# A segment sum over 400,000 edges: eight chunks moved from gathering to counting, and one operation for three weight parts

## Chip, cores and metric

One core of a Trainium2 chip runs the whole kernel. The metric is device time in microseconds (us). Of the kernel before, three timed runs gave 4982.99, 4986.41 and 4995.05; the median is 4986.41.

## What is computed

A graph has 12,500 nodes with 64 features and 400,000 edges, sorted by their target `dst`. Every edge brings a message to its target: the source node's features times `node_w`, plus the edge's own 64 attributes times `review_w`, both times the edge's weight. The messages are summed by target, added to the node, and the result is normalised over its 64 features.

```python
h = feat_src @ node_w.T
rf = review_feat @ review_w.T
m = (h[src_idx] + rf) * edge_w
out = segment_sum(m, dst_idx, num_segments=N_DST)
x = layernorm(x + out, axis=-1)
```

The two matrix products are linear, so the kernel sums the weighted raw features by target first and multiplies the 12,500 sums by the weights at the end.

## The kernel before

The edges are cut at `COUNTED_FROM`. Those ahead of it are *gathered*, those behind it are *counted*; the two ways run interleaved on the same engines.

**Gathered: 88 chunks of 3200 edges** (25 tiles of 128). For a chunk SyncE (SP) loads `src`, `dst`, the weights and the edge attributes, and GpSimd (POOL) issues 25 indirect DMAs (`gather_chunk`, L366), each of which fetches the 256-byte rows of x for 128 edges into `rows`. Four slots of `rows` are in use, so the gather of chunk c + 4 starts when VectorE has freed the slot of chunk c. VectorE makes for each of the 25 tiles a weighted one-hot over 128 targets (`scatter`, L441), and TensorE multiplies `rows` by it, 25 fp32 products into one *window* of PSUM (`window_ps`, L839; each has two passes in the trace, so 50 matmuls). VectorE adds the window to `sums` (L453).

**Counted: 925 tiles of 128 edges in 52 groups** of 18 tiles (7 in group 0). No row of x is fetched. For each tile VectorE makes two one-hots: `hot_key` (L495, 128 x 686), which says which block of 128 nodes the source lies in and which of seven target slots the edge goes to, and `hot_lo` (L497), the source's place within its block, times the edge's weight. The weight is cut in three bf16 parts W0, W1 and W2, so `hot_lo` has three planes of 128 x 128. TensorE multiplies them: six bf16 matmuls of 343 columns for a tile (L881), which leaves in `count_ps` how much of every node each target slot gets. There are two such PSUM buffers and three buffers for the one-hots. ScalarE copies `count_ps` to `counts` (L744). At the group's end TensorE multiplies `counts` by the table of x held in SBUF (`sum_x`, L896, 98 products or 196 matmuls), ScalarE reads the result (`x_sums`, L759, once in a group), and two small products and an addition (L904, L905, L911, L531) bring the group's 126 slots into `sums`.

**Preparing a group.** `prepare` packs key, low part and weight parts of 18 tiles in rows of `packed`; TensorE turns them into columns in the middle of the sum over x of the group before (`turn_cols`, L855 to L859); ScalarE copies them to `cols` (L728); then VectorE's `begin_hot` makes `hot_rel` (L510, L514) and the first three hot tiles of the next group. W0 comes from `g_w` and stands last in `cols`.

**Order.** Each engine's program is written out by hand in steps, and a hardware loop runs over rounds of them. One step has one group and one or two chunks. TensorE's order in a step is: window of the first chunk, `turn_slots`, the 18 counting tiles, window of the second chunk if there is one, `multiply_slots`, sum over x. `STEPS = (2, 1, 2, 1, 2)` gives the chunks of a round's five steps; nine rounds are run, then six steps with two chunks (`LAST_STEPS`), two more chunks, and the last two (`LATE_CHUNKS`). On VectorE the hot tiles of the next group's start stand ahead of the scatter of the next step's first chunk. The last stage multiplies `sums` by the weights in 15 blocks of up to eight rows of 128 nodes, adds x, normalises and stores; the blocks that the last two chunks can reach come late.

Of the kernel before, what the change touches and what calls it, by code (L numbers as in the profile page):

```python
# [25 lines left out]
ALU = mybir.AluOpType  # L26
# [8 lines left out]
P = 128  # L35
# [7 lines left out]
GT = 18  # L43
HOT_BUFS = 3
SPAN = 7
CHUNKS = 88
STEPS = (2, 1, 2, 1, 2)
LAST_STEPS = (2, 2, 2, 2, 2, 2)
LATE_CHUNKS = 2
LN_EPS = 1e-5  # L50

# [1 line left out]
def build(nc, x, src, dst, attr, weight, node_w, review_w, out):  # L53
# [4 lines left out]
    GROUP = GT * P  # L58
    COUNTED_FROM = CHUNKS * CHUNK
    COUNTED = (EDGES - COUNTED_FROM) // P  # L60
# [4 lines left out]
    HI = (NODES - 1) // P + 1  # L65
# [23 lines left out]
    blocks = [(h, until - h) for h, until in zip(edges, edges[1:])]  # L89
    BLOCKS = len(blocks)  # L90
# [4 lines left out]
    BY_P = NODES // P  # L95
    G_DST_DMAS = 1 + (GT - 1) // GT0 + 1

    with ExitStack() as ctx:
# [20 lines left out]
        x_tab = sb("x_tab", [P, HI, F])  # L119
# [4 lines left out]
        hi_lo = sb("hi_lo", [GT, 2, P], I32)  # L124
        tile_first = sb("tile_first", [GT, 1])
        w_cut = sb("w_cut", [GT, 2, P], BF16)
        KEY, LO, W1, W2, REL, W0 = range(6)
        packed = sb("packed", [GT, W0, P])
        cols = sb("cols", [P, W0 + 1, GT])
        slot_rel = sb("slot_rel", [NS, 1])  # L130
# [3 lines left out]
        hot_lo = [sb(f"hot_lo{b}", [P, 3, P], BF16) for b in range(HOT_BUFS)]  # L134
# [8 lines left out]
        count16 = sb("count16", [P, HI * SPAN], F16)  # L143
# [109 lines left out]
        stored = sem("stored")  # L253
# [53 lines left out]
        @block.sync  # L307
        def _(sp):
            def load_src(c, s):
                sp.dma_start(src_sb[s][:, :], by_partition(src, c)).then_inc(src_landed[s], 16)  # L310

            def load_rest(c, s):
                sp.dma_start(dst_sb[s][:, :], by_partition(dst, c)).then_inc(edge_landed[s], 16)
                sp.dma_start(w_sb[s][:, :], by_partition(weights, c)).then_inc(edge_landed[s], 16)
                sp.dma_start(rows[:, s, :, F:2 * F],
                             attr[bass.ds(c * CHUNK, CHUNK), :].rearrange("(p k) f -> p k f", k=TILES)
                             ).then_inc(edge_landed[s], 16)

            def load_chunk(c, s, r):

                sp.wait_ge(slot_free[s], r + 1)
                load_src(c, s)
                load_rest(c, s)

            for s in range(SLOTS):
                load_src(s, s)
            sp.dma_start(dst_i[:, 0, :], dst.rearrange("(c e) -> c e", e=CHUNK)).then_inc(dst_loaded, 16)

            sp.dma_start(g_dst[1:GROUPS, :, :], dst[COUNTED_FROM + GT0 * P:EDGES].rearrange(
                "(g t e) -> g t e", t=GT, e=P)).then_inc(g_dst_loaded, 16)  # L330
            for t0 in range(0, GT, GT0):
                n = min(GT0, GT - t0)
                sp.dma_start(g_dst[0:1, t0:t0 + n, :], dst[COUNTED_FROM:COUNTED_FROM + n * P].rearrange(
                    "(a t e) -> a t e", a=1, e=P)).then_inc(g_dst_loaded, 16)
            sp.dma_start(w_both[:, 0:F], node_w).then_inc(w_loaded, 16)
            sp.dma_start(w_both[:, F:2 * F], review_w).then_inc(w_loaded, 16)
            for s in range(SLOTS):
                load_rest(s, s)
            each_chunk(sp, SLOTS, CHUNKS, load_chunk)

            sp.wait_ge(tables_ready, 1)
            with sp.If(is_narrow(sp) == 0):
                each_chunk(sp, CHUNKS, ALL_CHUNKS, load_chunk)
            for n, b in enumerate(early + late):
                h0, j = blocks[b]
                if n < ACT_BLOCKS:
                    sp.wait_ge(act_scaled, n + 1)
                else:
                    sp.wait_ge(pool_scaled, n - ACT_BLOCKS + 1)
                whole = min(j, BY_P - h0)  # L350
                sp.dma_start(out[h0 * P:(h0 + whole) * P, :].rearrange("(h l) f -> l h f", l=P),
                             x_tab[:, h0:h0 + whole, :]).then_inc(stored, 16)
                if whole < j:
                    sp.dma_start(out[BY_P * P:NODES, :], x_tab[0:NODES - BY_P * P, BY_P, :]).then_inc(stored, 16)
            sp.wait_ge(stored, 16 * (BLOCKS + (BY_P < HI)))

        @block.gpsimd
        def _(pool):
# [50 lines left out]
        def _(dve):  # L409
# [77 lines left out]
            def make_hot(g, tiles):  # L487

                n0 = tiles_before(g)
                for t in tiles:  # L490
                    h = t % HOT_BUFS

                    if t >= HOT_BUFS:
                        dve.wait_ge(counted, n0 + t - HOT_BUFS + 1)
                    dve.tensor_scalar(hot_key[h][:, :], count16[:, :], cols[:, KEY, t:t + 1], None, ALU.is_equal)  # L495
                    for i, part in enumerate((W0, W1, W2)):
                        made = dve.tensor_scalar(hot_lo[h][:, i, :], count16[:, 0:P], cols[:, LO, t:t + 1],  # L497
                                                 cols[:, part, t:t + 1], ALU.is_equal, ALU.mult)
                    made.then_inc(hot_ready, 1)

            def begin_hot(g):
# [146 lines left out]
            for a in range(2):  # L648
                made = dve.tensor_scalar(w_t[:, a * F:(a + 1) * F], w_t_ps[:, 0:F], w_mean[:, 0:1], None, ALU.subtract)
# [352 lines left out]
```

## Time and profile before

| | us |
|---|---|
| median of three timed runs | 4986.41 |
| profiled execution, span of the core | 4978.1 |
| TensorE matmuls busy | 2706.6 (54%) |
| TensorE weight loads busy | 2036.4 (41%) |
| VectorE busy | 1848.4 (37%) |
| ScalarE busy | 832.4 (17%) |
| GpSimd busy | 2097.5 (42%) |
| mean granted clock of TensorE | 0.722 of full speed |

The timed median lies 8.3 us above the span. In the rows, an instruction or a group of merged ones stands with its start, its length, and in brackets the idle time of its engine ahead of it with what ended that. A matmul's end is modelled, its start is recorded. "issue" means that the profile shows nothing for which the engine waited, "remote" that the releasing instruction isn't among the records.

### The profile page before, as it was taken

To read this page: it belongs to the slowest core of one execution; us is meant where nothing else is said; L and a number is where in the kernel's file an instruction comes from. 1 tells how busy PE (TensorE), PEld (TensorE's weight loads), DVE (VectorE), ACT (ScalarE), POOL (GpSimd) and SP (SyncE) were. 2 spreads that over 40 slices of the span, in tenths; PEclk is the share of its full clock that TensorE was granted. 3 is DMA by queue.
4 is the path that set the end of the run, shared out by engine and by line. 5 is a ranking of instruction groups with operands and counts; after the bars stand their busy time and mean duration, and the time that the engine had idled before them with its cause. 6 is when DMAs were issued, how large, how long until landed. Compare 5 with 4: busy or idle time off the path is not lost.

```text
span 4978.1 us, 63532 instructions
## 1 busy us (share of the span) xinstructions
PE 2706.6 (54%) x22003; PEld 2036.4 (41%) x22004; DVE 1848.4 (37%) x7016; ACT 832.4 (17%) x1327; POOL 2097.5 (42%) x2223
## 2 busy tenths in 40 slices
PE   0555555545655545555456555555554556455465
PEld 0343444434443434444344434344443444344345
DVE  3333333423442333333334424333333344333344
ACT  0111111111121111121111211111111112111112
POOL 7343343443334443444433344434444333544432
PEclk9776777767776767777667767677776777667677
DMA  4111121111111111211111211112111112112111
GB/s 98 37 34 37 34 42 38 34 36 38 37 38 38 34 35 38 41 38 34 35 38 35 42 37 35 34 38 42 38 34 35 37 36 42 37 34 43 36 35 38
DMA packets 531458, 192.11 MB, mean 39 GB/s; under 512 B 489893, under 2 KB 495772, under 8 KB 530975
## 3 DMA queue, kind: packets, MB, share of 16 engines
q1 hardware_dynamic: 334128, 80.80, 8.6%
q0 software_dynamic: 70400, 72.23, 6.6%
q10 hardware_dynamic: 126623, 34.94, 3.2%
q8 instruction: 198, 3.24, 0.3%
q14 instruction: 109, 0.89, 0.1%
HBM read 184.60 MB, written 3.20 MB: 38 GB/s over the span
## 4 chain that ended last, share of the span: by engine, by line
PE 43%; another core or an unknown queue 28%; issue 21%; DVE 4%; ACT 2%; DVEq 1%; ACTq 1%; POOLq 0%; POOL 0%
PE x_sums_ps L896 15%; PE count_ps L881 15%; PE window_ps L839 11%; ACT counts L744 2%; DVE scatter L441 1%; DVE hot_lo L497 1%; PE attr_ps L873 1%; ACTq L771 0%; PE turn_ps L858 0%; PE turn_ps L855 0%; DVEq L422 0%; DVEq L425 0%; DVE hot_key L495 0%; PE count_ps L924 0%
## 5 line engine op out<-in xcount | busy, mean ns | idle before, releaser
L366 POOL DMA_INDIRECT rows<-x,src x2200 | 2088.8, 949 | 2791.5 <-DMA src<-src 2146.3
L881 PE MATMUL count_ps<-hot_key,hot_lo 128*128 128x343 bf16 x5550 | 1157.4, 361 | 1294.2 <-ACT counts L744 839.0
L896 PE MATMUL x_sums_ps<-counts,x_tab 128*64 128x126 f32 (+1 forms) x10192 | 865.5, 302 | 790.2 <-issue 775.0
L881 PEld LDWEIGHTS count_ps<-hot_key,hot_lo 128*128 128x128 bf16 x5550 | 570.1, 113 | 1726.5 <-issue 1092.5
L896 PEld LDWEIGHTS x_sums_ps<-counts,x_tab 128*64 128x64 f32 x10192 | 692.5, 154 | 948.4 <-issue 927.3
L744 ACT ACTIVATE counts<-count_ps 128x686 f32<-128x686 f32 x925 | 737.3, 802 | 1784.9 <-remote 1335.6
L495 DVE TENSOR_SCALAR hot_key<-count,cols 128x686 bf16<-128x686 f16 x925 | 377.8, 408 | 1550.8 <-remote 1272.3
L441 DVE TENSOR_SCALAR scatter<-column,dst_left,w 128x128 f32<-128x128 f32 x2200 | 588.3, 347 | 576.2 <-PE window_ps L839 503.0
L497 DVE TENSOR_SCALAR hot_lo<-count,cols 128x128 bf16<-128x128 f16 x2775 | 721.7, 323 | 4.9 <-issue 4.9
L839 PE MATMUL window_ps<-scatter,rows 128*128 128x128 f32 x4400 | 563.1, 289 | 85.2 <-issue 55.4
L839 PEld LDWEIGHTS window_ps<-scatter,rows 128*128 128x128 f32 x4400 | 535.0, 200 | 120.9 <-issue 108.8
L510 DVE TENSOR_TENSOR hot_rel<-column,cols 128x126 f32<-128x126 f32 (+1 forms) x52 | 15.2, 292 | 645.1 <-issue 441.8
L873 PEld LDWEIGHTS attr_ps<-hot_rel,g_attr 128*128 128x128 f32 x926 | 189.0, 228 | 45.1 <-issue 9.5
L726 ACT ACTIVATE slot_rel<-turn_ps,slot_no 126x1 f32<-126x1 f32 (+1 forms) x52 | 13.6, 262 | 979.2 <-remote 625.3
L873 PE MATMUL attr_ps<-hot_rel,g_attr 128*128 128x14 f32 x926 | 155.2, 243 | 12.6 <-remote 12.6
L759 ACT ACTIVATE x_sums<-x_sums_ps 128x126 f32<-128x126 f32 (+1 forms) x52 | 14.3, 276 | 881.9 <-PE x_sums_ps L896 881.9
L734 ACT ACTIVATE slot_rows<-x_sums_ps 126x128 f32<-126x128 f32 x52 | 14.4, 278 | 400.8 <-PE x_sums_ps L905 400.8
L448 DVE TENSOR_SCALAR dst_left<-dst_left 128x25 f32<-128x25 f32 x88 | 15.8, 180 | 146.8 <-PE window_ps L839 146.8
L531 DVE TENSOR_TENSOR sums<-sums,turn_ps 128x128 f32 x52 | 15.0, 289 | 76.2 <-PE turn_ps L911 43.0
L430 DVE TENSOR_SCALAR dst_left<-dst,lo_all 128x25 f32<-128x25 int32 x88 | 22.3, 254 | 50.2 <-issue 50.2
L405 POOL TENSOR_TENSOR x_tab<-x_tab,counts 128x512 f32<-128x512 f32 (+2 forms) x8 | 5.9, 748 | 79.7 <-DVE counts L573 79.6
L855 PE MATMUL turn_ps<-tile_first,spread 18*126 18x1 f32 (+1 forms) x104 | 19.4, 253 | 33.7 <-DVE packed L484 33.7
(112 smaller groups left out, 557.5 us busy)
## 6 DMA issues: line engine op xcount, KB each, us to landing
rows<-edge_attr SPq DMA_DIRECT2D x88, 800.0 KB
rows<-x,src POOLq DMA_INDIRECT x2200
g_attr<-edge_attr ACTq DMA_DIRECT2D x51, 576.0 KB
out<-x_tab SPq DMA_DIRECT2D x11, 256.0 KB
counts<-dst SPq DMA_DIRECT2D x1, 1562.5 KB
src<-src SPq DMA_DIRECT2D x88, 12.5 KB, 1.7
dst<-dst SPq DMA_DIRECT2D x88, 12.5 KB
w<-edge_weight SPq DMA_DIRECT2D x88, 12.5 KB
```

Source lines behind the costliest of these rows:

```text
L366: pool.indirect_dma_start(out=rows[:, s, k, 0:F], out_offset=None, in_=x, in_offset=bass.IndirectOffsetOnAxis(ap=src_sb[s][:, k:k + 1].bit ...
L430: dve.tensor_scalar(dst_left[:, :], dst_sb[s][:, :], lo_all[:, bass.ds(c, 1)], None, ALU.subtract).then_inc(left_ready, 1)
L441: made = dve.tensor_scalar(scatter[:, q % PART_BUFS, i, :], column[:, :], dst_left[:, k:k + 1], w_sb[s][:, k:k + 1], ALU.is_equal, ALU.mult)
L448: dve.tensor_scalar(dst_left[:, :], dst_left[:, :], float(WIN), None, ALU.subtract).then_inc(left_ready, 1)
L495: dve.tensor_scalar(hot_key[h][:, :], count16[:, :], cols[:, KEY, t:t + 1], None, ALU.is_equal)
L497: made = dve.tensor_scalar(hot_lo[h][:, i, :], count16[:, 0:P], cols[:, LO, t:t + 1], cols[:, part, t:t + 1], ALU.is_equal, ALU.mult)
L744: act.activation(counts[:, :, t * SPAN:(t + 1) * SPAN].rearrange("p (a h) d -> p a h d", a=2), count_ps[t % 2][:, :, 0:HALF].rearrange("p ...
L839: done = pe.matmul(window_ps[:, 0:WIN], rows[:, s, k, :], scatter[:, q % PART_BUFS, i, :], start=(k == 0), stop=(k == TILES - 1))
L855: pe.matmul(turn_ps[0:nt * SPAN, REL_COL:REL_COL + 1], spread[0:nt, 0:nt * SPAN], tile_first[0:nt, 0:1], start=True, stop=True)
L873: pe.matmul(attr_ps[0:(until - t) * F, t * SPAN:until * SPAN], g_attr[:, t:until, :].rearrange("p t f -> p (t f)"), hot_rel[:, t:until, :] ...
L881: last = pe.matmul(count_ps[b][:, a, 0:HALF], hot_lo[h][:, i, :], hot_key[h][:, a * HALF:(a + 1) * HALF], start=(i == 0), stop=(i == 2))
L896: done = pe.matmul(x_sums_ps[half * F:(half + 1) * F, 0:ns], x_tab[:, hi, :], counts[:, hi, 0:ns], start=(hi < 2), stop=(hi >= HI - 2))
```

## The change

`CHUNKS` goes from 88 to 80: 200 of the 2200 gather instructions go, and 1125 tiles are counted in 63 groups (9 tiles in group 0) where 925 were in 52. The steps of a round become ten with 12 chunks, eight of them with one chunk; with 63 groups the loop runs six rounds, and two steps of two chunks follow. The columns are reordered so that W1, W2 and W0 lie side by side, and the three `tensor_scalar` that made the planes of `hot_lo` become one `scalar_tensor_tensor` over 3 x 128 elements: the counter spread over the planes is compared with the low part and multiplied by the weight part of the plane, spread over 128 elements. The late blocks become rows 59 to 64, the last block is row 97 alone, and the store skips an empty range.

```diff
-CHUNKS = 88
-STEPS = (2, 1, 2, 1, 2)
-LAST_STEPS = (2, 2, 2, 2, 2, 2)
+CHUNKS = 80
+STEPS = (1, 1, 1, 1, 2, 1, 1, 1, 1, 2)
+LAST_STEPS = (2, 2)
...
-        KEY, LO, W1, W2, REL, W0 = range(6)
+        KEY, LO, REL, W1, W2, W0 = range(6)
...
                 whole = min(j, BY_P - h0)
-                sp.dma_start(out[h0 * P:(h0 + whole) * P, :].rearrange("(h l) f -> l h f", l=P),
-                             x_tab[:, h0:h0 + whole, :]).then_inc(stored, 16)
+                if whole:
+                    sp.dma_start(out[h0 * P:(h0 + whole) * P, :].rearrange("(h l) f -> l h f", l=P),
+                                 x_tab[:, h0:h0 + whole, :]).then_inc(stored, 16)
...
                     dve.tensor_scalar(hot_key[h][:, :], count16[:, :], cols[:, KEY, t:t + 1], None, ALU.is_equal)
-                    for i, part in enumerate((W0, W1, W2)):
-                        made = dve.tensor_scalar(hot_lo[h][:, i, :], count16[:, 0:P], cols[:, LO, t:t + 1],
-                                                 cols[:, part, t:t + 1], ALU.is_equal, ALU.mult)
+                    made = dve.scalar_tensor_tensor(
+                        hot_lo[h][:, :, :], count16[:, 0:P].unsqueeze(1).to_broadcast([P, 3, P]), cols[:, LO, t:t + 1],
+                        cols[:, W1:W0 + 1, t].unsqueeze(2).to_broadcast([P, 3, P]), ALU.is_equal, ALU.mult)
                     made.then_inc(hot_ready, 1)
```

## Rows read from the trace of the kernel before

**Rows 1.** The page, costliest groups: busy us, mean ns of one, idle before.

```profile
L366 POOL DMA_INDIRECT rows<-x,src x2200 | 2088.8, 949 | 2791.5 <-DMA src<-src 2146.3
L881 PE MATMUL count_ps<-hot_key,hot_lo 128*128 128x343 bf16 x5550 | 1157.4, 361 | 1294.2 <-ACT counts L744 839.0
L495 DVE TENSOR_SCALAR hot_key<-count,cols 128x686 bf16<-128x686 f16 x925 | 377.8, 408 | 1550.8 <-remote 1272.3
L497 DVE TENSOR_SCALAR hot_lo<-count,cols 128x128 bf16<-128x128 f16 x2775 | 721.7, 323 | 4.9 <-issue 4.9
```

**Rows 2.** Stretches of one step: length, PE, PEld, DVE, ACT, POOL busy (count), clock, DMA.

```profile
2108.40:2139.60 31.20, 10.45 (x58) 6.03 (x56) 7.98 (x30) 5.62 (x7) 23.69 (x25) 0.65 0.26 52
2139.60:2152.80 13.20, 10.10 (x50) 6.36 (x50) 6.33 (x24) 6.54 (x9) 0.00 (x0) 0.65 0.01 3
2152.80:2165.50 12.70, 11.80 (x204) 11.37 (x204) 7.62 (x33) 1.54 (x6) 0.00 (x0) 1.00 0.24 51
```

**Rows 3.** The same view, a gather over the sum over x.

```profile
2058.00:2091.00 33.00, 10.77 (x92) 6.51 (x89) 9.19 (x36) 0.41 (x2) 23.97 (x25) 0.63 0.24 51
```

**Rows 4.** ScalarE's reads of x_sums: timeline of one round, then all, then the last.

```profile
1989.11 0.28 ACT L759 ACTIVATE x_sums<-x_sums_ps 128x126 f32<-128x126 f32 x1 [21.80 <-PE x_sums_ps L896]
...
2098.92 0.28 ACT L759 ACTIVATE x_sums<-x_sums_ps 128x126 f32<-128x126 f32 x1 [27.51 <-PE x_sums_ps L896]
...
2165.26 0.28 ACT L759 ACTIVATE x_sums<-x_sums_ps 128x126 f32<-128x126 f32 x1 [5.11 <-PE x_sums_ps L896]
...
2269.75 0.28 ACT L759 ACTIVATE x_sums<-x_sums_ps 128x126 f32<-128x126 f32 x1 [23.14 <-PE x_sums_ps L896]
...
2337.19 0.28 ACT L759 ACTIVATE x_sums<-x_sums_ps 128x126 f32<-128x126 f32 x1 [5.11 <-PE x_sums_ps L896]
...
2443.57 0.28 ACT L759 ACTIVATE x_sums<-x_sums_ps 128x126 f32<-128x126 f32 x1 [21.34 <-PE x_sums_ps L896]
...
L759 ACT ACTIVATE x_sums<-x_sums_ps x52: 213/277/278, 156.3 to 4891.9; 128x126 f32<-128x126 f32 x51, 128x49 f32<-128x49 f32 x1
...
L759 ACT ACTIVATE x_sums<-x_sums_ps x7: 277/277/278, 4267.0 to 4891.9; 128x126 f32<-128x126 f32 x7
```

**Rows 5.** Timeline of TensorE, first window of a round.

```profile
2447.85 8.05 PE L839 MATMUL window_ps<-scatter,rows 128*128 128x128 f32 x50 [4.32 <-issue]
```

**Rows 6.** Timeline: window behind a two-chunk step; then hot tiles, scatter, window behind one-chunk.

```profile
2099.33 5.84 PE L839 MATMUL window_ps<-scatter,rows 128*128 128x128 f32 x50 [0.45 <-issue]
...
2160.82 0.40 DVE L495 TENSOR_SCALAR hot_key<-count,cols 128x686 bf16<-128x686 f16 x1
...
2161.79 0.40 DVE L495 TENSOR_SCALAR hot_key<-count,cols 128x686 bf16<-128x686 f16 x1
...
2164.02 6.50 DVE L441 TENSOR_SCALAR scatter<-column,dst_left,w 128x128 f32<-128x128 f32 x25
...
2165.78 6.17 PE L839 MATMUL window_ps<-scatter,rows 128*128 128x128 f32 x50 [0.56 <-DVE scatter L441]
```

**Rows 7.** Groups by shape: scalar_tensor_tensor of the last stage, and an operand spread by zero steps.

```profile
L514 DVE TENSOR_TENSOR hot_rel<-hot_rel,cols 128x126 f32<-128x126 f32 x51 | 15.0, 293 | 1.7
...
L549 DVE SCALAR_TENSOR_TENSOR x_tab<-x_total,x_tab 128x512 f32<-128x512 f32 x11 | 8.0, 726 | 0.9 <-DVE sums L531 0.9
...
L549 DVE SCALAR_TENSOR_TENSOR x_tab<-x_total,x_tab 128x192 f32<-128x192 f32 x2 | 0.7, 349 | 0.0
```

**Rows 8.** Timeline of clear counting: ScalarE's reads and VectorE's hot_key.

```profile
2044.93 0.80 ACT L744 ACTIVATE counts<-count_ps 128x686 f32<-128x686 f32 x1 [0.22 <-PE count_ps L881]
2044.93 0.40 DVE L495 TENSOR_SCALAR hot_key<-count,cols 128x686 bf16<-128x686 f16 x1
...
2045.94 0.80 ACT L744 ACTIVATE counts<-count_ps 128x686 f32<-128x686 f32 x1 [0.21 <-PE count_ps L881]
```

**Rows 9.** Timeline of the head: VectorE under the first gathers, a tile's count behind them.

```profile
81.63 0.31 DVE L497 TENSOR_SCALAR hot_lo<-count,cols 128x128 bf16<-128x128 f16 x1 [1.11 <-issue]
...
146.35 1.90 PE L881 MATMUL count_ps<-hot_key,hot_lo 128*128 128x343 bf16 x6
```

More of the change, by code:

```diff
@@ L350, in _ @@
                 whole = min(j, BY_P - h0)
-                sp.dma_start(out[h0 * P:(h0 + whole) * P, :].rearrange("(h l) f -> l h f", l=P),
-                             x_tab[:, h0:h0 + whole, :]).then_inc(stored, 16)
+                if whole:
+                    sp.dma_start(out[h0 * P:(h0 + whole) * P, :].rearrange("(h l) f -> l h f", l=P),
+                                 x_tab[:, h0:h0 + whole, :]).then_inc(stored, 16)
                 if whole < j:
                     sp.dma_start(out[BY_P * P:NODES, :], x_tab[0:NODES - BY_P * P, BY_P, :]).then_inc(stored, 16)
-            sp.wait_ge(stored, 16 * (BLOCKS + (BY_P < HI)))
+            sp.wait_ge(stored, 16 * (sum(h0 < BY_P for h0, _ in blocks) + (BY_P < HI)))
         @block.gpsimd
```

## Prediction, made before the changed kernel was run

> **What bounds the kernel now.** I began with the page's parts 1 and 5. No engine is near full: the gathers of GpSimd (POOL) are 2200 instructions, 25 for a chunk, each 0.95 us, and TensorE's counting matmuls, the next line, are busy for 1157 us [rows 1]. A mean over the run hides the point, so the second view is the table of stretches through one step. Under a chunk's gather (31.2 us) TensorE starts 58 matmuls; in the 13.2 us behind it 50; in the 12.7 us of the sum over x 204 [rows 2]. A gather that falls on the sum over x does the same: 92 matmuls in 33 us [rows 3]. So the time is made of two kinds of stretch: clear ones, and those under a gather, in which TensorE almost stands still whatever its work is. Why it stands the trace doesn't say; that it does is enough for the sum.
>
> The third view gives the price list. ScalarE reads x_sums once in a group, so the distance between two such reads is one step [rows 4]. The round shown goes two, one, two, one, two chunks: 109.8, 66.3, 104.5, 67.4 and 106.4 us. I take 67.0 for a one-chunk step. The first step of a round holds the loop's branch: TensorE is idle for 4.32 us there and the window takes 8.05 us [rows 5], against 5.84 us, 0.41 us behind the x_sums read, in an ordinary step [rows 6]; that is 5.9 us a round. Nine rounds last from 156.3 to 4267.0, 456.7 each, which leaves (456.7 - 134.0 - 5.9) / 3 = 105.6 for a two-chunk step; the six two-chunk steps behind the loop take 104.15 each [rows 4]. A chunk's marginal price is therefore 38.6 us (about 6 of window and 32 of standstill), a group's 28.4.
>
> **The mix of steps.** The changed kernel has 6 rounds of eight one-chunk and two two-chunk steps, then two two-chunk steps. At the prices above a round is 8 x 67.0 + 2 x 105.6 + 5.9 = 753.1, the whole 4518.6 + 208.3 = 4726.9. Before, the same stretch is 4735.6 (156.3 to 4891.9) [rows 4]. So the exchange alone is worth -8.7: eight chunks and three loop passes out (-309 and -18), eleven groups in (+313), and four of the cheaper steps behind the loop become steps of a round (+6). 200 gather instructions go, and so do eight chunks' loads on SP's queue; ScalarE's queue gets the loads of eleven more groups. Both queues issue beside TensorE's work, in steps of unchanged length, so I cost them at nothing; were one of them late, the stretch behind it would grow, and I have no sign of that in a one-chunk step.
>
> **A price that the list hides.** Every one-chunk step of before follows a two-chunk step, whose long sum over x gives VectorE time to make the hot tiles and the scatter ahead. Of the new kernel's 48 one-chunk steps 36 follow a one-chunk step. There VectorE is late: it gets the columns in the middle of the sum over x, makes three hot tiles at 0.97 each, and starts the scatter at 2164.02; TensorE's window ends 6.69 us after the x_sums read (start at 2165.78, 6.17 long). Behind a two-chunk step it is 0.41 + 5.84 = 6.25 [rows 6]. That is +0.44 for 36 steps: +15.8.
>
> **The one operation.** For each tile three tensor_scalar become one scalar_tensor_tensor over 384 elements. The four operations of a tile take 0.97 us start to start, though their durations add up to 1.38 (0.41 and three of 0.32): each overlaps the next by 0.10 [rows 1, 6]. So the three cost 0.67. The nearest rows of the new operation have 192 elements (0.349 us) and 512 (0.726) [rows 7]; on a line between them 384 take 0.575, less 0.10 of overlap 0.47. The bounds are the two rows, 0.25 and 0.63. The operand spread by a step of zero costs nothing that shows: hot_rel's two such operations take 0.29 us [rows 7]. I take 0.47, a saving of 0.20 a tile.
>
> What is it worth? Not VectorE's 0.20 x 1125 us. In a clear counting stretch ScalarE's reads follow each other at 1.01 us, each 0.80 long, and VectorE's hot_key starts at the same instant as the read: it too waited for TensorE's `counted` [rows 8]. The pace is TensorE's tile, then ScalarE's read, with two PSUM buffers; VectorE, at 0.97, has just enough time. A faster VectorE changes nothing there, nor under a gather, where TensorE is the late one. The saving counts only where VectorE's queue runs into the scatter. Before a window that follows a one-chunk step it brings the scatter forward by 3 x 0.20 = 0.6, of which TensorE can use what its own pace leaves, 6.17 - 5.84, and hardly more: 0.35. That is 48 steps (36 and the 12 two-chunk ones behind a one-chunk step): -16.8. Before the second window of a two-chunk step only one tile's saving counts, 14 x 0.2 = -3. With the upper bound, 0.63, the windows would gain 0.12 each, -6 in all. With the lower they gain no more than with 0.47.
>
> VectorE: DVE Perf Modes of the Trainium skill (The perf-mode tier table, and the errata table above it) speaks against this edit: a one-source bf16 operation may run four results a cycle, a two-source one at most two and in fp32 one, and its formula gives 0.28 us for the three operations and 0.46 for the new one. By it VectorE would lose 0.18 a tile, and the windows 48 x 0.54 = 26 us where I have a gain of 17. The measured 0.67 for the three contradicts the first figure; no row here shows the new form.
>
> **Head and tail.** Group 0 has 9 tiles for 7. It ends behind the first four gathers, when a tile costs TensorE 1.9 us [rows 9]: +4. The order of columns (REL ahead of W1) moves nothing. The blocks of the last stage stay 15, two of them late with six rows for five; at most 2 us, taken as 0. The store of an empty block is skipped.
>
> **Sum.** -8.7 + 15.8 - 19.8 + 4 = -8.7. The profiled execution (4978.1) becomes 4969.4. The median of the timed runs lies 8.3 above the span, which I keep: 4978.
>
> **Rivals.**
> 1. *VectorE is part of the standstill* (faster). At the head, under the first gathers, a hot_lo starts after 1.11 us of idle that nothing in the profile explains [rows 9]. If that happens in the steps too, two instructions fewer a tile shorten each standstill: 1 us for 62 groups, 4916. Against it: in the steps VectorE starts each time with the release by TensorE.
> 2. *The one operation is slower than the three* (slower). It decides from 0.70 us: then VectorE needs more than the 1.01 of a tile. At twice the slope of the rows, 384 x 2 x 1.18 ns is 0.9, less overlap 0.8: nine clear tiles of 62 groups pay 0.10 each, 56, the windows 48 x 0.4 = 19, and the gain of 20 is gone: 5073. The page named above would put the slowing at the windows alone, 5024. For it: bf16 and fp16 operands, which no scalar_tensor_tensor row has. Against: 0.726 for 512 elements.
> 3. *A chain of one-chunk steps is dearer than its pieces*, as the loads of a group then come every 67 us without a pause. From +0.5 us for each of 48 steps the kernel is slower by 0.3%; at +0.8, 5016.
> 4. *The one operation does not save anything*: +20 on the sum, 4998, still within 0.3%.
>
> **How the numbers follow.** About 0.3% (15 us) is what a measurement of this kernel can tell from no change. My sum: 0.57, between 4960 and 4994, of which 0.18 below 4971. Rival 1: 0.19, 4895 to 4960. Rival 2: 0.08. Rival 3: 0.10, of which 0.08 beyond 0.3%. Rival 4: 0.06. So faster 0.37, same 0.47, slower 0.16. The likeliest case's own range is 4960 to 4994; for 8 in 10 it has to reach into rivals 1 and 3: 4935 to 5008.
>
> **What would show it.** One-chunk steps of 67.0 to 67.4 between x_sums reads, two-chunk ones of 105; six idle stretches of about 4 us instead of nine; the new operation at 0.55 to 0.6 us long and the period of hot_key ahead of a window at 0.77; the window behind a one-chunk step at 5.9 instead of 6.17; the reads in clear counting still at 1.01. The prediction is wrong if that last pace moves, if a chunk's standstill is not 29 to 32 us any more, or if the one-chunk step leaves 66.5 to 67.8: 0.3 us there is 14 us in all.

## The result, and the profile after

The changed kernel takes 4740.57 us (median, 4733.61 to 4764.11), the kernel before 4989.44 beside it: a ratio of 0.951 (0.949 to 0.954). The forecast was 4978, with 4935 as its lower end. The change is faster by 249 us where I had summed up 9.

In later runs the kernel before took 4924 to 4993 us on three chips of this kind and 2814 to 2819 us on three others, so each run below is read against the kernel before on its own chip, and "with the standstill" or "without it" says which kind of chip it was.

The page of the changed kernel, two of its costliest groups (busy us, mean ns of one, idle before) and its chain; the first two answer to [rows 1]:

```profile
L367 POOL DMA_INDIRECT rows<-x,src x2000 | 1988.2, 994 | 2673.1 <-DMA src<-src 2086.4 <-issue 586.7
...
L497 DVE SCALAR_TENSOR_TENSOR hot_lo<-count,cols 128x384 bf16<-128x384 f16 x1125 | 686.4, 610 | 0.0
...
PE 56%; another core or an unknown queue 22%; issue 16%; ACT 4%; DVE 2%; DVEq 0%; POOL 0%; ACTq 0%; POOLq 0%
```

The new operation lasts 0.61 us. The line to look at is the first: the same gather instruction, with the same work, now lasts 994 ns where it lasted 949. Nobody had touched it.

One step of the changed kernel (one chunk behind one chunk), under its gather, behind it, and in the sum over x; columns as in [rows 2]:

```profile
core 0: us, PE busy (x) PEld busy (x) DVE busy (x) ACT busy (x) POOL busy (x), PEclk, DMA share, GB/s
2158.63:2191.22 32.59, 16.83 (x89) 9.70 (x89) 11.31 (x24) 9.63 (x12) 25.27 (x25) 0.68 0.25 49
2191.22:2200.37 9.15, 5.94 (x26) 3.73 (x26) 1.76 (x7) 3.40 (x6) 0.00 (x0) 0.50 0.04 10
2200.37:2211.84 11.47, 11.47 (x202) 11.27 (x198) 6.23 (x24) 0.41 (x2) 0.00 (x0) 0.98 0.24 54
```

The gather is 1.4 us longer than in [rows 2], and TensorE starts 89 matmuls under it where it started 58. What is left for the stretch behind it takes 9.2 us. The sum over x is as before. The time was gained in the counting tiles that lie under a gather, the place to which the forecast gave nothing.

The reads of x_sums of the same steps; they answer to [rows 4]:

```profile
2026.70 0.28 ACT L760 ACTIVATE x_sums<-x_sums_ps 128x126 f32<-128x126 f32 x1 [5.11 <-PE x_sums_ps L897]
2085.98 0.28 ACT L760 ACTIVATE x_sums<-x_sums_ps 128x126 f32<-128x126 f32 x1 [5.11 <-PE x_sums_ps L897]
2148.95 0.28 ACT L760 ACTIVATE x_sums<-x_sums_ps 128x126 f32<-128x126 f32 x1 [5.11 <-PE x_sums_ps L897]
2212.15 0.28 ACT L760 ACTIVATE x_sums<-x_sums_ps 128x126 f32<-128x126 f32 x1 [5.11 <-PE x_sums_ps L897]
2315.37 0.28 ACT L760 ACTIVATE x_sums<-x_sums_ps 128x126 f32<-128x126 f32 x1 [18.38 <-PE x_sums_ps L897]
```

One-chunk steps of 59.3, 63.0 and 63.2 us, a two-chunk step of 103.2; the price list had 67.0 and 105.6. Over the whole run, the counting of a group (first count matmul to last, mean over the groups of 18 tiles) went from 47.2 to 43.9 us. For 62 groups that is 205 us, nearly all of the 216 by which the two spans differ (4978.1 and 4762.4).

### The profile page after: what moved, and what is told of

Its sections match the earlier page's. It is cut to its first block, busy times and chain, and to the rows that moved or that the text cites. A ratio compares the mean times of both kernels' runs of the same rounds, so it can differ in the third digit from the quotient of the medians.

```text
span 4762.4 us, 69733 instructions
## 1 busy us (share of the span) xinstructions
PE 2948.5 (62%) x25313; PEld 2219.9 (47%) x25314; DVE 1864.9 (39%) x5496; ACT 1005.4 (21%) x1593; POOL 1996.9 (42%) x2023
## 4 chain that ended last, share of the span: by engine, by line
PE 56%; another core or an unknown queue 22%; issue 16%; ACT 4%; DVE 2%; DVEq 0%; POOL 0%; ACTq 0%; POOLq 0%
PE count_ps L882 26%; PE x_sums_ps L897 17%; PE window_ps L840 10%; ACT counts L745 4%; DVE hot_lo L497 1%; PE attr_ps L874 1%; PE turn_ps L859 0%; PE turn_ps L856 0%; PE x_sums_ps L906 0%; PE x_sums_ps L905 0%; DVE scatter L442 0%; DVE hot_key L496 0%; DVE x_tab L550 0%; DVE x_tab L563 0%
## 5 line engine op out<-in xcount | busy, mean ns | idle before, releaser
L367 POOL DMA_INDIRECT rows<-x,src x2000 | 1988.2, 994 | 2673.1 <-DMA src<-src 2086.4
L882 PE MATMUL count_ps<-hot_key,hot_lo 128*128 128x343 bf16 x6750 | 1480.6, 373 | 1271.0 <-ACT counts L745 637.9
L882 PEld LDWEIGHTS count_ps<-hot_key,hot_lo 128*128 128x128 bf16 x6750 | 702.1, 115 | 1849.0 <-issue 1068.4
L745 ACT ACTIVATE counts<-count_ps 128x686 f32<-128x686 f32 x1125 | 896.5, 802 | 1952.9 <-remote 1090.7
L496 DVE TENSOR_SCALAR hot_key<-count,cols 128x686 bf16<-128x686 f16 x1125 | 467.3, 415 | 1696.7 <-remote 1031.9
L497 DVE SCALAR_TENSOR_TENSOR hot_lo<-count,cols 128x384 bf16<-128x384 f16 x1125 | 686.4, 610 | 0.0
L442 DVE TENSOR_SCALAR scatter<-column,dst_left,w 128x128 f32<-128x128 f32 x2000 | 523.0, 352 | 254.8 <-PE window_ps L840 237.4
L840 PE MATMUL window_ps<-scatter,rows 128*128 128x128 f32 x4000 | 490.4, 284 | 72.3 <-issue 61.6
L840 PEld LDWEIGHTS window_ps<-scatter,rows 128*128 128x128 f32 x4000 | 475.6, 199 | 92.2 <-issue 89.6
L874 PEld LDWEIGHTS attr_ps<-hot_rel,g_attr 128*128 128x128 f32 x1126 | 238.4, 236 | 48.7 <-issue 6.4
```

The lines of the kernel that those rows point to most:

```text
L367: pool.indirect_dma_start(out=rows[:, s, k, 0:F], out_offset=None, in_=x, in_offset=bass.IndirectOffsetOnAxis(ap=src_sb[s][:, k:k + 1].bit ...
L442: made = dve.tensor_scalar(scatter[:, q % PART_BUFS, i, :], column[:, :], dst_left[:, k:k + 1], w_sb[s][:, k:k + 1], ALU.is_equal, ALU.mult)
L497: made = dve.scalar_tensor_tensor(hot_lo[h][:, :, :], count16[:, 0:P].unsqueeze(1).to_broadcast([P, 3, P]), cols[:, LO, t:t + 1], cols[:, ...
L745: act.activation(counts[:, :, t * SPAN:(t + 1) * SPAN].rearrange("p (a h) d -> p a h d", a=2), count_ps[t % 2][:, :, 0:HALF].rearrange("p ...
L840: done = pe.matmul(window_ps[:, 0:WIN], rows[:, s, k, :], scatter[:, q % PART_BUFS, i, :], start=(k == 0), stop=(k == TILES - 1))
L874: pe.matmul(attr_ps[0:(until - t) * F, t * SPAN:until * SPAN], g_attr[:, t:until, :].rearrange("p t f -> p (t f)"), hot_rel[:, t:until, :] ...
```

## Experiments

Theory A: under a gather every instruction of VectorE is dear, and what counts is how many it runs for a tile (two for four). Theory B: it is the kind of the operation, one with a second tensor input, that counts. Rival to both: the gain is in the mix of steps.

**The operation alone, and the mix alone.** The first kernel is the kernel before with the one operation and its order of columns, 88 chunks; the second is the changed kernel with three operations:

```diff
-                    made = dve.scalar_tensor_tensor(
-                        hot_lo[h][:, :, :], ...
+                    for i, part in enumerate((W0, W1, W2)):
+                        made = dve.tensor_scalar(hot_lo[h][:, i, :], count16[:, 0:P], cols[:, LO, t:t + 1],
+                                                 cols[:, part, t:t + 1], ALU.is_equal, ALU.mult)
```

> The kernel before with the one operation alone (88 chunks, 52 groups). If the gain lies in the one operation, the counting phase under a gather falls from 47.2 to about 43.9 us as in the changed kernel: 51 groups x 3.3 = 168, with the windows about 175, so 4815. If it lies in the new mix of steps (one-chunk steps in a row), this stays within 20 of the kernel before, 4970 to 4990.

> The changed kernel with three tensor_scalar for the one operation (80 chunks, 63 groups). If the gain lies in the one operation: counting phases at 47 us, the time as my sum had it without the operation, 4990 to 5005. If it lies in the mix: about 4750.

Measured: the operation alone 4770.61 us, ratio 0.957 (0.954 to 0.959), 45 us better than expected; the mix alone 5004.39, ratio 1.002 (1.001 to 1.004), as expected. The gain is the operation's. On the mix it is worth five points, on the old mix four.

**Number or kind.** The third kernel makes the three parts with three scalar_tensor_tensors of 128 elements, the fourth adds two one-element operations to the changed kernel, between hot_key and the one operation:

```diff
+                    for i, part in enumerate((W1, W2, W0)):
+                        made = dve.scalar_tensor_tensor(
+                            hot_lo[h][:, i, :], count16[:, 0:P], cols[:, LO, t:t + 1],
+                            cols[:, part, t:t + 1].to_broadcast([P, P]), ALU.is_equal, ALU.mult)
```
```diff
+                    for i in range(2):
+                        dve.tensor_scalar(filler[:, 2 * h + i:2 * h + i + 1], count16[:, 0:1], 1.0, None, ALU.mult)
```

> The changed kernel with three scalar_tensor_tensor of 128 elements for the one of 384: the same kind of operation with two inputs, but as many VectorE instructions as before. If the number of VectorE instructions under a gather sets how far counting gets there (theory A), the counting phase goes back to about 47 us and the time to 4950 to 5000. If the kind of operation sets it (theory B: tensor_scalar in its fast mode disturbs, or is disturbed by, GpSimd at the memory port they share), the phase stays at about 44 us and the time at 4735 to 4780.

> The changed kernel with two idle tensor_scalar of one element added for each tile, so as many VectorE instructions as before and the one operation kept. Theory A: counting phases back to about 47 us, 4950 to 5000. Theory B: phases at 44 us, 4735 to 4780 (the two take some 0.1 us of VectorE, which has room in a tile).

Measured, one run each: 5062.21 and 4700.5 us, beside 4993; both lie outside the ranges of both theories. Four instructions for a tile are again there in the kernel with fillers, and it is no slower than the changed one (4734 to 4764): theory A falls. The kind alone is dearer, not cheaper: theory B in that form falls too. But the trace of the three shows where to look. A gather in the timeline of GpSimd:

```profile
2085.66 1.13 POOL L367 DMA_INDIRECT rows<-x,src  x1 [29.43 <-DMA src<-src]
2087.09 14.21 POOL L367 DMA_INDIRECT rows<-x,src  x1 [0.30 <-issue]
2101.61 0.94 POOL L367 DMA_INDIRECT rows<-x,src  x1 [0.30 <-issue]
2102.86 0.95 POOL L367 DMA_INDIRECT rows<-x,src  x1 [0.30 <-issue]
```

The same gather of the same kernel in the table of stretches, cut where the instructions start to flow (columns as above):

```profile
2085.66:2101.30 15.64, 15.58 (x105) 9.38 (x104) 14.82 (x55) 11.78 (x15) 15.34 (x2) 1.00 0.28 56
2101.30:2130.03 28.73, 11.00 (x88) 6.79 (x85) 2.48 (x12) 1.38 (x4) 21.71 (x24) 0.64 0.25 47
```

While VectorE runs its operations one behind the other (busy 14.82 of 15.64 us), one gather instruction takes 14.21 us and no other is begun. In that time TensorE counts at its clear pace, 105 matmuls with a granted clock of 1.00. As soon as VectorE pauses, gather instructions come every 1.25 us, and TensorE makes 88 matmuls in 28.7 us, of the short kind of the sum over x, at 0.64. So the standstill does not belong to the chunk's step. It belongs to the gather instructions, at that pace.

The page "SBUF — State Buffer" of the Trainium skill (SBUF: two separate sides) names a lock: VectorE and GpSimd share a pair of ports, and whoever starts first holds it for the whole instruction. It says that a DMA issued from GpSimd can't write its descriptors while VectorE is in a 2-port mode; an operation with two inputs in SBUF it has blocking only a GpSimd operation that reads SBUF. A hold beside two-input operations is what the trace shows, but one of 14.21 us, in which 48 instructions of VectorE start, is more than a lock for one instruction; that this lock is the cause is not shown.

In the changed kernel the hold is a small one. Its timeline under a gather, VectorE's new operation and GpSimd:

```profile
2166.32 0.60 DVE L497 SCALAR_TENSOR_TENSOR hot_lo<-count,cols 128x384 bf16<-128x384 f16 x1
2166.54 1.20 POOL L367 DMA_INDIRECT rows<-x,src  x1 [0.30 <-issue]
...
2168.04 0.94 POOL L367 DMA_INDIRECT rows<-x,src  x1 [0.30 <-issue]
...
2169.19 0.61 DVE L497 SCALAR_TENSOR_TENSOR hot_lo<-count,cols 128x384 bf16<-128x384 f16 x1
2169.29 1.33 POOL L367 DMA_INDIRECT rows<-x,src  x1 [0.30 <-issue]
2170.92 0.94 POOL L367 DMA_INDIRECT rows<-x,src  x1 [0.30 <-issue]
```

A gather instruction that meets the operation takes 1.20 or 1.33 us, one that doesn't 0.94. The two are longer by 0.26 and 0.39 us, and when they began the operation had 0.38 and 0.51 us left. Counted over the run, 310 of 2000 take over 1.1 us, where it was 11 of 2200.

This gives **theory C**: what makes TensorE stand still is GpSimd's gather instructions coming every 1.25 us. The one operation holds some of them up by 0.3 us, TensorE gets tiles through, each brings another such operation, which holds up another instruction. Within the changed kernel it looks like that. Its 42 one-chunk steps with one gather and no loop branch, sorted by the gather's length: the third with the shortest gathers (mean 31.8 us) lasts 65.1 us, the middle one (32.4) 63.9, the one with the longest (33.2) 62.5. A longer gather goes with a shorter step. That is a correlation, since more tiles under a gather also hold it up more; the next runs separate the two.

**Away from VectorE.** Four kernels: the changed kernel with a one-input operation of the same 384 elements (it leaves out the two low parts of the weights); the kernel before with three or seven one-element memsets on GpSimd behind each gather instruction; the kernel before with an unused scalar_tensor_tensor of 128 elements for each tile.

```diff
-                    made = dve.scalar_tensor_tensor(
+                    made = dve.tensor_scalar(
                         hot_lo[h][:, :, :], count16[:, 0:P].unsqueeze(1).to_broadcast([P, 3, P]), cols[:, LO, t:t + 1],
-                        cols[:, W1:W0 + 1, t].unsqueeze(2).to_broadcast([P, 3, P]), ALU.is_equal, ALU.mult)
+                        cols[:, W0, t:t + 1], ALU.is_equal, ALU.mult)
```
```diff
+                pool.wait_ge(paused, c * (3 * TILES) + 1)
...
                     ).then_inc(gathered[s][k // PER_PART], 16)
+                    for i in range(3):
+                        pool.memset(pause[:, k, i, :], 0.0).then_inc(paused, 1)
```
```diff
+                    dve.scalar_tensor_tensor(filler[:, h, :], count16[:, 0:P], cols[:, LO, t:t + 1],
+                                             cols[:, W0:W0 + 1, t].to_broadcast([P, P]), ALU.is_equal, ALU.mult)
```

> The changed kernel with its one operation made a one-input one: a tensor_scalar of the same 384 elements, with the one-hot scaled by the first part of the weight in all three places (so the two low parts of the weights are left out of the sums; the amount of work of every engine is otherwise that of the changed kernel). Theory C (the three-input operation holds up GpSimd, whose gather instructions then come less densely, and that is what lets TensorE go on): without it the gathers come every 1.25 us again, and the time goes back to that of the mix with three operations, 5004 us, at least 4950. Theory A (what counts is that VectorE has two instructions per tile and not four): as the changed kernel or better, 4700 to 4745 us.

> The kernel before, with VectorE's work as it was (three operations, 88 chunks), and three memsets of one element on GpSimd behind every gather instruction. They should make the distance of gather instructions some 1.55 us in place of 1.25, and a gather some 39 us long. Theory C: the standstill under the gather shrinks as in the changed kernel, 4700 to 4800 us, with more than 8 tiles counted under a gather. Theory A, or any theory in which VectorE's own time is the cause: no gain, 4989 us or more, up to 5150 if a longer gather only makes the standstill longer.

> As the paced kernel before, with seven memsets behind every gather instruction: a distance of some 1.9 to 2.0 us, a gather of 48 to 50 us, still shorter than a one-chunk step. Theory C: at least as fast as with three memsets, 4600 to 4750 us, unless the gather of the second chunk of a two-chunk step (105 us for two gathers) comes late, which would show as waits for rows. Theory A: 4989 to 5250 us.

> The kernel before with one more operation per tile: a scalar_tensor_tensor of 128 elements into a buffer that nobody reads, between hot_key and the three tensor_scalars. VectorE then has five instructions and some 0.35 us more per tile. Theory C: it blocks GpSimd as the one operation does, a little shorter (0.35 for 0.61 us per tile), so the gathers thin out and the time falls to 4780 to 4900 us. Theory A: slower than before, 5000 to 5060 us (18 tiles a group by up to 0.35 us where VectorE is near the pace of a tile).

Measured: 2623.33, 2909.28, 3197.36 and 2805.21 us, and the kernel before, on the same chip, 2813.81. No expectation covers that. These runs tell nothing of A against C, because there was no standstill to shorten. A gather of the first of them (taken on yet another chip of this kind, 2628.42 us) in the table of stretches:

```profile
1159.41:1190.61 31.20, 30.05 (x344) 25.36 (x342) 19.52 (x66) 10.56 (x19) 23.88 (x25) 1.00 0.25 49
```

Here are 25 gather instructions in 31.2 us as in [rows 2], 344 matmuls beside them for 58 (many of them the short ones of the sum over x, which TensorE now reaches under the gather), the clock at 1.00. So the gather as such does not stop TensorE; on some chips it does, on others not. The chain of such a run of the kernel with the extra operation says POOL 75%: without the standstill 88 gathers are the bound, and pauses between them only cost.

Was it the chip? The changed kernel as it is, once more:

> The changed kernel as it is. The four runs before this one went to another chip of the same kind, on which the kernel before takes 2813.81 us and no standstill shows. Theory C1 (the standstill belongs to the chip on which the change was timed, and the kernel's own bound is GpSimd's gathers, 8 fewer in 88): on a chip without the standstill 2620 to 2680 us beside 2814 for the kernel before (2814 less 8 chunks of 25 gather instructions at 1.25 us, 250 us, plus what the port costs: up to 0.3 us on a third of 2000 instructions, 60 us); on the chip with it 4740 us beside 4989. Rival C2 (the mix alone pays nothing even without the standstill): 2790 us or more there.

Measured: 4742.12 beside 4989.88, ratio 0.951. The standstill was back, with the first result to 0.1%. The three kernels that tell A from C, a second time:

> The same kernel as e5_one_input (one operation with one input and 384 elements; the two low parts of the weights left out), for a chip on which the kernel before takes 4989 us. There theory C expects 4950 to 5010 us (gathers every 1.25 us again, standstill as before), theory A (the count of VectorE's instructions, or its time, decides) 4700 to 4745 us. On a chip without the standstill it would repeat 2623 us.

> The same kernel as e6_paced_before (kernel before, three memsets of one element behind each gather instruction), for a chip with the standstill. Theory C: gather instructions further apart let TensorE count more than 8 tiles under a gather, 4700 to 4850 us. Theory A: 4989 us or more. If the distance does not grow (on the chip without the standstill a gather took 31.7 us with the memsets, not the expected 39), it tests nothing, and the time should be 4989 to 5090 us.

> The same kernel as e8_extra_stt (kernel before with one scalar_tensor_tensor of 128 elements more per tile), for a chip with the standstill. Theory C: 4780 to 4900 us, with a gather longer than 31.05 us and more than 8 tiles under it. Theory A: 5000 to 5060 us.

Measured: 2628.42, 2915.2 and 2804.94, the kernel before 2818.64: again a chip without the standstill, each within 0.2% of its first time. A third time, now with a pause that is long enough (three memsets had moved the distance of gather instructions only from 1.25 to 1.27, since they fill a gap of 0.30 us that GpSimd has anyway):

```diff
                     ).then_inc(gathered[s][k // PER_PART], 16)
+                    pool.wait_ge(paused, c * TILES + (k + 1))
+                    pool.sem_inc(pauses, 1)
+                    pool.memset(pause[:, :], 0.0).then_inc(paused, 1)
```

(`pause` has 440 bf16 elements in a partition; the wait is for the memset before, and no engine other than GpSimd takes part.)

> The changed kernel with a one-input tensor_scalar of 384 elements in place of the one operation (the two low parts of the weights left out), a third time, for a chip with the standstill (kernel before 4989 us). Theory C (the second tensor input holds up GpSimd, thinner gathers relieve TensorE): 4950 to 5010 us, gather 31.1 us long, 8 tiles under it. Theory A (number or time of VectorE's instructions): 4700 to 4745 us. Without the standstill 2623 to 2630 us again.

> The kernel before with one memset of 440 elements on GpSimd behind each gather instruction, meant to set them 1.6 us apart in place of 1.25 (a gather of some 40 us), VectorE untouched. On a chip with the standstill, theory C: the standstill loses tiles to the gather as in the changed kernel, 4650 to 4800 us, 10 or more of 18 tiles under a gather. Theory A: no gain, 4989 to 5250 us. On a chip without it GpSimd is the bound and the time rises from 2816 to some 3600 us (2200 instructions at 1.6 us and the head).

> The kernel before with a scalar_tensor_tensor of 128 elements more per tile, a third time, for a chip with the standstill. Theory C: 4780 to 4900 us and gathers longer than 31.05 us. Theory A: 5000 to 5060 us. Without the standstill 2805 us again.

Measured, with the standstill (kernel before 4924.25): the one-input operation 4878.49, ratio 0.991 (0.988 to 0.994); **the paced kernel before 3664.99, ratio 0.744** (0.742 to 0.747); the extra operation 4949.24, ratio 1.006 (1.003 to 1.008). The paced kernel, timeline of GpSimd:

```profile
1459.68 0.95 POOL L368 DMA_INDIRECT rows<-x,src  x1 [0.16 <-POOL pause L374]
1460.63 0.63 POOL L374 MEMSET pause<- 128x440 bf16 x1
1461.43 0.95 POOL L368 DMA_INDIRECT rows<-x,src  x1 [0.16 <-POOL pause L374]
```

The same kernel in the table of stretches, one gather and the 18 counting tiles within it:

```profile
1451.66:1492.27 40.61, 37.12 (x361) 28.67 (x362) 28.55 (x101) 15.73 (x24) 36.68 (x50) 0.92 0.29 58
1456.13:1476.16 20.03, 19.14 (x125) 11.72 (x125) 17.04 (x60) 13.51 (x18) 18.07 (x25) 0.95 0.33 64
```

VectorE's program is that of the kernel before. The gather instructions are 1.6 to 1.75 us apart, and 361 matmuls are started under a gather for 58, part of them again those of the sum over x. The counting of a group takes 19.4 us in the mean for 47.2. The standstill is gone, not shortened, and the bound is now GpSimd: the page's chain says

```profile
POOL 63%; issue 36%; POOLq 1%; PE 0%; DMA 0%; DVE 0%; ACT 0%; DVEq 0%
```

and TensorE waits for rows, in this window 4.4 to 5.6 us ahead of each ten matmuls:

```profile
1436.61 2.47 PE L845 MATMUL window_ps<-scatter,rows 128*128 128x128 f32 x10 [4.41 <-DMA rows<-x,src]
1444.64 2.48 PE L845 MATMUL window_ps<-scatter,rows 128*128 128x128 f32 x10 [5.55 <-DMA rows<-x,src]
1452.72 2.48 PE L845 MATMUL window_ps<-scatter,rows 128*128 128x128 f32 x10 [5.61 <-DMA rows<-x,src]
```

That thinning out GpSimd's gather instructions ends the standstill, with VectorE's program as it was, is thereby shown; it came out stronger than expected, since I had 4650 to 4800 and a standstill that shrinks. This run alone doesn't tell the distance from the memset and the wait that stand in it: the kernel with one-element memsets, at 1.27 us, was never timed with the standstill. The fillers' trace helps, since no memset stands in it. One of its gathers:

```profile
1010.25 1.26 POOL L368 DMA_INDIRECT rows<-x,src  x1 [25.22 <-DMA src<-src]
1011.82 1.00 POOL L368 DMA_INDIRECT rows<-x,src  x1 [0.30 <-issue]
1013.12 1.36 POOL L368 DMA_INDIRECT rows<-x,src  x1 [0.30 <-issue]
1014.79 1.31 POOL L368 DMA_INDIRECT rows<-x,src  x1 [0.31 <-issue]
...
1010.20:1030.00 19.80, 15.76 (x106) 10.05 (x105) 14.55 (x53) 11.34 (x15) 15.78 (x14) 1.00 0.35 64
```

The first 12 distances of this gather are 1.48 us in the mean, and TensorE counts at a granted clock of 1.00; the group is done in 22.4 us. So it goes in 13 of that kernel's 62 groups: 22.0 to 25.2 us, with first distances of 1.44 to 1.51. In the 45 groups of 38 us and more they are 1.29 to 1.41 (four lie between), and in the kernel before 1.25 to 1.27. As faster counting itself brings more holds, this goes with theory C without proving it, but the standstill goes away at such distances with no memset too.

The one-input kernel has the same number and size of operations as the changed one and gets 1 point of its 5. Its ratio is 0.001 below theory C's range (4950 to 5010 beside 4989), and far from theory A's (0.942 to 0.951). The extra operation missed theory C's 4780 to 4900: it holds up only 40 of 2200 gather instructions, so it tests little. The one-input kernel's gather row among the groups by line (mean ns in the middle) is that of before again:

```profile
L367 POOL DMA_INDIRECT rows<-x,src x2000 | 1903.0, 952 | 2872.1 <-DMA src<-src 2285.2 <-issue 587.0
```

and that of the kernel with the one operation alone, 88 chunks, is that of the changed kernel:

```profile
L366 POOL DMA_INDIRECT rows<-x,src x2200 | 2174.6, 988 | 2492.6 <-DMA src<-src 1847.4 <-issue 645.2
```

The durations of the other kernels come from the same row of theirs:

| kernel, with the standstill | ratio to the kernel before | gather instruction, mean ns | of them over 1.1 us | mean distance, us | counting of a group, us |
|---|---|---|---|---|---|
| before | 1 | 949 | 11 of 2200 | 1.25 | 47.2 |
| mix, three operations | 1.002 | 950 | 22 of 2000 | 1.26 | 47.4 |
| mix, one-input operation | 0.991 | 952 | 9 of 2000 | 1.26 | 45.9 |
| before, extra operation | 1.006 | 957 | 40 of 2200 | 1.26 | 46.5 |
| one operation, 88 chunks | 0.957 | 988 | 293 of 2200 | 1.29 | 43.5 |
| changed | 0.951 | 994 | 310 of 2000 | 1.30 | 43.9 |
| changed, two fillers | 0.941 | 999 | 274 of 2000 | 1.31 | 39.2 |
| before, paced | 0.744 | 956 | 13 of 2200 | 1.64 | 19.4 |

(Distances are start to start within a gather. The last column of the one-input, the extra and the paced kernel comes from a chip whose kernel before is 1.3% faster than the other's; ratios are each against their own.) The kernels at 1.25 or 1.26 us lie within 1.1% of the kernel before, those at 1.29 to 1.31 at 0.94 to 0.96, the one at 1.64 at 0.744. Within the middle group the mean distance doesn't order them: the changed kernel on its second chip has 1.31 as well. The fillers' 39.2 us is a mean of two kinds of group, the 13 without a standstill and 45 of 44.3 us, as long as those of the changed kernel. The three scalar_tensor_tensors (1254 ns, ratio 1.014) do not fit a mean: in 8 of the first 14 one-chunk steps nearly the whole gather is put off until the counting is over and then stands in the way of the sum over x, which takes 41 us for 11.5, so nothing is won. Why a single extra operation of 128 elements holds up so few instructions, and three in a row so many, is left open.

**How far apart.** Three distances in the changed kernel (the same pause with 440, 250 and 120 elements):

> The changed kernel with a memset of 440 elements on GpSimd behind each gather instruction (as in the paced kernel before: 1.63 us apart, a gather of 40.4 us). If this removes the standstill here too, GpSimd is the bound: 80 gathers of 40.4 us and 110 us around them, 3340 us (3310 to 3400), that is the paced kernel before less 8 gathers, 323 us. Rival: with the one operation the port is taken longer and the memsets and gathers stretch each other, 3400 to 3550 us.

> The same with a memset of 250 elements: some 1.44 us apart, a gather of 36 us. If the standstill goes at any clear thinning (graded: the further apart, the less of it, and 1.44 is half-way), 2990 us if it is gone wholly (80 times 36 and 110 around), up to 3700 if half of it is left. Threshold rival (the standstill is there in full below 1.5 us): 4600 to 4750 us.

> The same with a memset of 120 elements: some 1.31 us apart, a gather of 33 us. Graded theory: much of the standstill left, 3900 to 4600 us. If the distance of 1.3 is already enough: 2750 us (80 times 33 and 110). Threshold rival: 4600 to 4750 us, as the changed kernel.

Measured: 3351.14, 3024.57 and 2887.31 us, the kernel before 2816.17: a chip without the standstill. They say only what pacing costs there. The first sum was right (3340): GpSimd is the bound, 80 gathers of 40.6 us. The shortest pause gave a distance of 1.41 and a gather of 35.0, not 33. How the standstill depends on a distance set by a pause between 1.31 and 1.64 us was not found (the fillers' groups above point to 1.4 to 1.45), nor was the changed kernel itself timed without the standstill (its one-input form took 2623 to 2628 us there beside 2814 to 2819, a ratio of 0.932). Of all kernels run with the standstill the paced kernel before is the fastest by far; without it, it would lose, by an estimate from the changed kernel with the same pause (1.190).

## Why the prediction was wrong

- **Two kinds of stretch**: right as a description, and it was not enough. I wrote that why TensorE stands still under a gather doesn't matter for the sum. It did: the price of a gather was taken for a property of the step, but it hangs on the distance of GpSimd's instructions, and the change moves that distance.
- **The mix of steps, with the hidden price**: right. (By the rows the loop's branch costs 6.1 us and not 5.9: 4.28 + 8.05 against 6.25. It moves the sum by less than 1 us.) Without the operation's gain the forecast is 4978 + 20 = 4998; the mix alone measured 1.0021 x 4989 = 5000.
- **The one operation, its length**: 0.61 us for 0.575. Ahead of a window two hot_keys start 0.84 apart (2208.54 and 2209.38, below) for a forecast 0.77, so it takes 0.53 for 0.47, within the bounds. The window behind a one-chunk step starts 0.42 behind the x_sums read and lasts 5.86, as forecast (5.9). The rule of "VectorE: DVE Perf Modes" of the Trainium skill that spoke against the edit gives an estimate of 0.46 us for the new operation; the row has 0.61, and the 26 us that the windows were to lose by it did not show.

```profile
2208.54 0.40 DVE L496 TENSOR_SCALAR hot_key<-count,cols 128x686 bf16<-128x686 f16 x1
2208.85 0.61 DVE L497 SCALAR_TENSOR_TENSOR hot_lo<-count,cols 128x384 bf16<-128x384 f16 x1
2209.38 0.40 DVE L496 TENSOR_SCALAR hot_key<-count,cols 128x686 bf16<-128x686 f16 x1
...
2212.57 5.86 PE L840 MATMUL window_ps<-scatter,rows 128*128 128x128 f32 x50 [0.46 <-issue]
```

- **Clear counting**: right, still 1.01 us a tile.
- **"Nor under a gather, where TensorE is the late one"**: this step failed. It looked for VectorE's own time on the path, and VectorE was indeed hardly ever late (2% of the chain). What it left out is the operation's effect on a third engine: it holds up GpSimd, GpSimd's instructions come less densely, and TensorE gains. Measured 3.3 us a group, 205 us in all, where the sum had 0.
- **Rival 1** (VectorE is part of the standstill, 1 us a group, 4916) had the place and the sign, and under a third of the size. Its cause, two instructions fewer, is refuted by the fillers (4700.5); the one-input kernel leaves at most 1 point for fewer and shorter instructions. Rivals 2 and 4 fell with the length and the gain, rival 3 with the mix.
- **The list of what would show it wrong** held: the one-chunk step left 66.5 to 67.8, and a gather lasts 32.2 us in the mean for 31.05.

The loop's idle stretch of 4.3 us [rows 5] is there in the changed kernel as well, 4.35 us (window at 2319.69), in fewer passes, as forecast.

## What to carry to other kernels

When one engine stands still beside another's work for no reason that the profile gives, find out what the standstill depends on before pricing anything by it; a pause of half a microsecond between the other engine's instructions is a short experiment, and on a chip with the standstill it was worth 25% here, against 5% of the change. An operation that gets a second tensor input is to be costed on GpSimd's instructions too, not only on VectorE's queue. And time on more than one chip: the bound of this kernel is TensorE's standstill on some and GpSimd's gathers on others, and the pause that wins 25% in the kernel before on the first costs 19% in the changed kernel on the second.

## What the runs showed of the hardware

- The same kernel takes 4924 to 4993 us on some chips and 2814 to 2819 us on others. The one-input kernel, traced on both kinds, has gathers of 31.1 and 31.2 us and counts a group in 45.9 or 17.8 us; the kernel with the extra operation in 46.5 or 21.0. Beside one gather TensorE's granted clock was 0.65 in the kernel before and 1.00 in the one-input kernel without the standstill.
- Where TensorE stands still, ScalarE learns late that a tile is done. The kernel before, ScalarE's count reads and TensorE's counting in one such stretch:

```profile
2116.43 1.06 PE L881 MATMUL count_ps<-hot_key,hot_lo 128*128 128x343 bf16 x6 [2.34 <-ACT counts L744]
2120.11 1.88 PE L881 MATMUL count_ps<-hot_key,hot_lo 128*128 128x343 bf16 x6 [2.61 <-issue]
...
2129.74 0.80 ACT L744 ACTIVATE counts<-count_ps 128x686 f32<-128x686 f32 x1 [9.78 <-remote]
2130.60 0.76 PE L881 MATMUL count_ps<-hot_key,hot_lo 128*128 128x343 bf16 x2 [8.38 <-ACT counts L744]
```

  Both engines take the tiles in order, 925 each. Counted off, the read at 2129.74 is that of the tile which by the profile was done at 2117.49, 12.3 us earlier; TensorE had begun its next tile at 2120.11; the profile knows no releaser ("remote"). As a matmul's end is modelled, the rows don't tell whether the result or only its signal was late. In the clear such a read begins 0.04 us behind the tile; in the kernel before 257 of 925 begin over 2 us behind it, in the paced kernel (1.64 us between gather instructions) none. In the other direction there is no delay: 0.05 us after the read's end at 2130.55 TensorE goes on.
- Beside a row of scalar_tensor_tensors of 128 elements on VectorE a gather instruction of GpSimd takes 14.21 us and more (44 of that kernel's 2000 over 10 us); a single one of 384 elements costs it 0.26 to 0.39 us. Tensor_scalars of the same tensors, 128 or 384 elements, cost it nothing that shows (9 to 22 of 2000 over 1.1 us).
- Why some chips show the standstill, and what delays a finished tile there, no run here tells.
